# The two products of x with the first layer's weights: two groups of 256-column matmuls, or one group of 512 columns over two shared banks

## The reference, cut to what matters

```
deg = jnp.sum(adj, axis=-1, keepdims=True)
agg = jnp.einsum('bij,bjf->bif', adj, x) / jnp.maximum(deg, EPS)
cat = jnp.concatenate([x, agg], axis=2)
out = jnp.einsum('bnf,of->bno', cat, W)      # W is 256 x 512
return jax.nn.relu(out)
...
x = _layernorm(x + _L0_gnn_ref(x, adj, L0_gnn_W), axis=-1)
```

## Time and profile before

| | us |
|---|---|
| median of 3 runs | 1295.62 |
| lowest, highest | 1294.18, 1297.25 |
| span of the profiled execution | 1294.0 |
| PE busy | 1276.6 (99%) |
| PE weight loads busy | 1173.7 (91%) |
| DVE busy | 1194.4 (92%) |
| ACT busy | 909.7 (70%) |
| POOL busy | 140.6 (11%) |

### The profile page before, as it was taken

One profiled execution on the slowest core, in us unless ns is written; L12 is line 12 of the kernel. 1 busy time (PEld: TensorE's weight loads), 2 busy tenths in 40 slices (PEclk: granted clock), 3 DMA queues, 4 the chain that ended last, 5 costly groups with the idle time before them and its releaser, 6 DMA issues.

```text
span 1294.0 us, 30492 instructions
## 1 busy us (share of the span) xinstructions
PE 1276.6 (99%) x10976; PEld 1173.7 (91%) x10976; DVE 1194.4 (92%) x3789; ACT 909.7 (70%) x2445; POOL 140.6 (11%) x265
## 2 busy tenths in 40 slices
PE   7999999999999999999999999999999999999997
PEld 7899999999999999999999999999999999999986
DVE  6988999999999999999999999999999999999996
ACT  7677767677667677677677676776676776776773
POOL 0100111101111101111101111011111011110011
PEclk9999999999999999999999999999999999999999
DMA  6110111110111110111100111101111101110000
GB/s 227 34 35 1 35 43 44 43 43 2 43 43 43 43 40 4 44 43 43 43 24 21 43 43 44 43 3 43 43 43 43 36 8 43 43 43 9 10 9 25
DMA packets 34307, 49.01 MB, mean 38 GB/s; under 512 B 7920, under 2 KB 16880, under 8 KB 34160
## 3 DMA queue, kind: packets, MB, share of 16 engines
q1 hardware_dynamic: 34160, 47.08, 11.6%
HBM read 38.68 MB, written 8.39 MB: 36 GB/s over the span
## 4 chain that ended last, share of the span: by engine, by line
PE 96%; DVE 1%; DMA 1%; ACT 1%; POOL 0%; issue 0%; SPq 0%; POOLq 0%; DVEq 0%
PE psum L1487 63%; PE psum L1501 13%; PE psum L1742 9%; PE psum L1700 8%; PE psum L1793 1%; PE psum L1796 1%; PE psum L1805 1%; DMA adjT_sb<-in_adjT 1%; PE psum L1816 0%; DMA v_sb<-in_w 0%; DVE bn L869 0%; POOL rstd L347 0%; POOL mv L344 0%; DVE x L903 0%; DVE w_l L840 0%
## 5 line engine op out<-in xcount | busy, mean ns | idle before, releaser
L536 ACT ACTIVATE work<-work,shift 128x256 f32<-128x256 f32 x512 | 253.7, 498 | 37.6 <-DVE shift L1032 37.6
L1051 DVE SCALAR_TENSOR_TENSOR work<-work,rsum,extra 128x256 f32<-128x256 f32 x512 | 216.7, 475 | 0.1
L1032 DVE CUSTOM_DVE_ANT_0 work<-psum,minus_big 128x256 f32<-128x256 f32 x512 | 189.4, 416 | 1.8 <-PE psum L1700 1.8
L387 ACT ACTIVATE work<-psum 128x512 f32<-128x512 f32 x256 | 138.1, 596 | 73.9 <-PE psum L1501 70.0
L387 ACT ACTIVATE sup_h<-psum 128x512 fp32r<-128x512 f32 x124 | 73.5, 593 | 142.6 <-PE psum L1487 142.4
L344 POOL TENSOR_TENSOR mv<-mv,eps 128x2 f32<-128x2 f32 x128 | 33.1, 259 | 1139.3 <-DVE mv L890 1139.3
L1487 PE MATMUL psum<-x2T_h,wqkv_h 128*128 128x256 f32 x512 | 146.3, 286 | 0.0
L1487 PE MATMUL psum<-x2T_l,wqkv_h 128*128 128x256 f32 x512 | 142.8, 279 | 0.0
L1487 PE MATMUL psum<-x2T_h,wqkv_l 128*128 128x256 f32 x512 | 142.8, 279 | 0.0
L1501 PE MATMUL psum<-ident,work 128*128 128x128 f32 x1024 | 129.0, 274 | 0.0
L1742 PE MATMUL psum<-work,v_sb 128*64 128x256 f32 x1024 | 124.6, 385 | 0.0
(11 more groups left out here) (156 smaller groups left out, 3738.9 us busy)
## 6 DMA issues: line engine op xcount, KB each, us to landing
xT_sb<-in_xT SPq DMA_DIRECT2D x32, 256.0 KB, 2.6
adjT_sb<-in_adjT SPq DMA_DIRECT2D x32, 256.0 KB, 3.0
adj_sb<-in_adj SPq DMA_DIRECT2D x32, 256.0 KB, 4.5
x_sb<-in_x SPq DMA_DIRECT2D x32, 256.0 KB, 4.7
out<-y_sb SPq DMA_DIRECT2D x32, 256.0 KB, 4.5
work<-in_wqkv SPq DMA_DIRECT2D x1, 1536.0 KB, 10.8
mask_row<-in_nodemask SPq DMA_DIRECT2D x32, 32.0 KB, 4.5
w_raw<-in_w SPq DMA_DIRECT2D x3, 256.0 KB, 7.0
```

What stands on the lines that cost most here:

```text
L387: return nc.scalar.activation(dst, src, ACT.Copy, scale=scale)
L536: last = nc.scalar.activation(prob[:, p % 2, i, h], prob[:, p % 2, i, h], ACT.Exp, bias=shift[:, p % 2, h, i:i + 1], scale=-1.0, accum_out ...
L1032: last = V_.tensor_tensor_reduce(out=prob[:, p % 2, i, h], in0=bank(SCORES[p] + h)[:, i * N:(i + 1) * N], in1=minus_big[:, g % 2, i], scal ...
L1051: last = V_.scalar_tensor_tensor(out=prob[:, p % 2, i, h], in0=prob[:, p % 2, i, h], scalar=rsum[:, p % 2, h, i:i + 1], in1=extra[:, g % 2 ...
```

## The change

The two products are computed together. The weights of own part and support already lie side by side (`w0` has 512 columns), so one matmul now has 512 moving columns: the first node tile writes bank 0, the second bank 2, each with the own part in columns 0 to 255 and the support in 256 to 511. `support0` and `self_product` become `front_product`, with one semaphore `pe_front` at its end. ACT's `self_copy` moves to right behind `sup0_hi`, ahead of `values`. Both copies and DVE's `sup0_lo` now read a half of either bank, and `sup0_lo` waits for `self_copy` too.

```
-        SUP0 = 0
-        SELF = 2
+        FRONT = (0, 2)
+        OWN, SUPPORT = 0, 1
...
+        def front(part):
+            return psum[:, FRONT[0]:FRONT[1] + 1:FRONT[1] - FRONT[0], part * F:(part + 1) * F]
...
                 else:
                     reuse(act, pe_gcn, once(g - 1))
-                    act.wait_ge(pe_sup0, once(g))
-                copy(sup_of(g)[0][:, :, :], halves(bank(SUP0))).then_inc(act_sup0, 1)
+                    act.wait_ge(pe_front, once(g))
+                copy(sup_of(g)[0][:, :, :], front(SUPPORT)).then_inc(act_sup0, 1)
...
-                act.wait_ge(pe_self, once(g))
+                act.wait_ge(pe_front, once(g))
                 reuse(act, dve_agg, once(g - 1))
-                copy(self_part[:, :, :], halves(bank(SELF))).then_inc(act_self, 1)
+                copy(self_part[:, :, :], front(OWN)).then_inc(act_self, 1)
...
                 sup_hi(2, s - 1)
                 sup0_hi(s)
+                self_copy(s)
                 values(s - 2)
-                self_copy(s)
...
                 dve.wait_ge(act_sup0, once(g))
-                lo(sup_of(g)[1][:, :, :], halves(bank(SUP0)), sup_of(g)[0][:, :, :]).then_inc(dve_sup0, 1)
+                dve.wait_ge(act_self, once(g))
+                lo(sup_of(g)[1][:, :, :], front(SUPPORT), sup_of(g)[0][:, :, :]).then_inc(dve_sup0, 1)
...
-            def support0(g, part):
+            def front_product(g, part):
                 if not live(g):
                     return
                 if part == HI:
-                    weights(g, W0)
+                    weights(g, W0 + 1)
                     reuse(pe, act_oT, nth(g - 3, 3))
                     pe.wait_ge(act_xT, once(g))
                     reuse(pe, dve_oT, nth(g - 3, 3))
+                    reuse(pe, act_self, once(g - 1))
+                    if g == 2:
+                        reuse(pe, act_x1T, once(g - 1))
+                        reuse(pe, dve_x1T, once(g - 1))
+                    else:
+                        reuse(pe, dve_scores, nth2(g - 2, 0, 1))
                 else:
                     pe.wait_ge(dve_xT, once(g))
-                last = nodes_product(bank(SUP0), fT_of(g), [w[:, :, F:2 * F] for w in w0], part)
+                x = fT_of(g)
+                for t in range(NT):
+                    last = product(bank(FRONT[t]), [(cut(x, A, k, block_of(t)), cut(w0, A, k)) for k in range(FT)],
+                                   LEFT_LATE[part], opens=part == HI, closes=part == LO)
                 if part == LO:
-                    last.then_inc(pe_sup0, 1)
+                    last.then_inc(pe_front, 1)
...
+                    if p == 3:
+                        pe.wait_ge(act_self, once(g + 2))
...
                 qk(s - 3, 2)
-                support0(s - 1, HI)
+                front_product(s - 1, HI)
                 hidden(1, s - 2, HI)
                 hidden(1, s - 2, LO)
-                support0(s - 1, LO)
-                self_product(s - 1)
+                front_product(s - 1, LO)
                 project_out(s - 4, HI)
```

More of the change, by code:

```diff
@@ L191, in graph_blocks_kernel @@
         pool_var, pool_rstd = sems("pool_var", 4), sems("pool_rstd", 4)
-        (pe_mask, pe_w0, pe_w3, pe_xT, pe_adjT, pe_sup0, pe_self, pe_agg, pe_x1T, pe_gcn, pe_x2T, pe_v,
+        (pe_mask, pe_w0, pe_w3, pe_xT, pe_adjT, pe_front, pe_agg, pe_x1T, pe_gcn, pe_x2T, pe_v,
          pe_qk, pe_scores, pe_probT, pe_pv, pe_y, pe_x3T, pe_proj3, pe_adjk, pe_gate_row, pe_gate_col) = (
-            sem(n) for n in ("pe_mask", "pe_w0", "pe_w3", "pe_xT", "pe_adjT", "pe_sup0", "pe_self", "pe_agg",
+            sem(n) for n in ("pe_mask", "pe_w0", "pe_w3", "pe_xT", "pe_adjT", "pe_front", "pe_agg",
                              "pe_x1T", "pe_gcn", "pe_x2T", "pe_v", "pe_qk", "pe_scores", "pe_probT", "pe_pv",
@@ L630, in first_graphs @@
                 sup0_hi(0)
+                self_copy(0)
                 x_hi(1)
                 degrees(0)
-                self_copy(0)
                 mask_bias(0)
@@ L665, in first_graphs @@
                 sup0_hi(2)
+                self_copy(2)
                 adj_exp(2)
@@ L668, in first_graphs @@
                 qk_hi(0, 1)
-                self_copy(2)
                 sup_hi(1, 1)
@@ L717, in first_graphs @@
                 exps(1, 1, 1)
-                self_copy(3)
                 sup_hi(2, 2)
                 sup0_hi(3)
+                self_copy(3)
                 values(1)
@@ L758, in first_graphs @@
                 hidden_hi(1, 3)
-                self_copy(4)
                 adj_exp(4)
@@ L763, in first_graphs @@
                 sup0_hi(4)
+                self_copy(4)
                 values(2)
@@ L1870, in first_graphs @@
             def first_graphs():
-                support0(0, HI)
-                support0(0, LO)
-                self_product(0)
+                front_product(0, HI)
+                front_product(0, LO)
                 aggregate(0, HI)
                 aggregate(0, LO)
-                support0(1, HI)
-                support0(1, LO)
-                self_product(1)
+                front_product(1, HI)
+                front_product(1, LO)
                 keep_busy(7, 4)
@@ L1894, in first_graphs @@
                 x1_transpose(1)
-                support0(2, HI)
                 support(2, 0, HI)
@@ L1900, in first_graphs @@
                 gcn_out(0, LO)
-                support0(2, LO)
-                self_product(2)
+                front_product(2, HI)
+                front_product(2, LO)
                 support(0, 1, HI)
@@ L1955, in first_graphs @@
                 project_out(0, HI)
-                support0(3, HI)
                 project_out(0, LO)
-                self_product(3)
                 support(2, 2, HI)
@@ L1962, in first_graphs @@
                 gcn_out(2, HI)
-                support0(3, LO)
+                front_product(3, HI)
+                front_product(3, LO)
                 gcn_out(2, LO)
```

## The result

| | before | after |
|---|---|---|
| median of the runs, us | 1295.62 | 1311.62 (1310.74 to 1312.26) |
| span of the profiled execution, us | 1294.0 | 1309.0 |
| gcn_out to gcn_out in a slot, median | 39.27 | 39.71 |

The change makes the kernel slower: the ratio, against the runs of before on the same chip, is 1.0119, with a 95% interval of 1.0107 to 1.0131. The forecast was 1303.3 us with a range up to 1310.0. The direction was right; the loss is twice the forecast, 16.0 us for 7.7 (15.0 us by the spans; 15.7 by the medians if a fourth run of before, which the result lists, is counted in: 1295.9). The granted clock is again full (0.999).

The account below looks back on a forecast made before the run. The prediction took PE's instruction list and stalls as the bound, with DVE also on the path. Product -0.9, wait +8.1 and start +0.5 gave +7.7 us, 1303.3 us from 1295.6, range 1296.5 to 1310.

Parts of the forecast that it names:

- What bounds the kernel: Whole span: PE, busy 99%, sets the time by its instruction list plus whatever makes it stand; DVE is also on the path.
- The loop over DVE's `x2_lo`: PE releases `gcn_out`, DVE needs 10.4 us to `x2_lo`, PE takes over at `qk(·,0)`; closes once a slot, about no slack.
- Product, -0.03 us a graph: First-layer products on PE: 12 matmuls of 512 columns replace 24 of 256, 2.76 for 2.79 us; -0.9 us over 32 graphs.
- The wait, +0.29 us a slot, +8.1: DVE's `sup0_lo` waits for ACT's second copy, 0.51 us late; PE then 0.29 us late, 8.1 us over 28 slots.
- The restart of 0.11 us: PE at `aggregate LO`: restarting after standing 0.18 us costs 0.11 us more, making it 0.29 us late.
- `hidden(1)` and all other groups, 0: `hidden(1)` ends about 0.9 us later, covered by idle time on ACT and DVE; moved work costs nothing.
- The start, +0.5 (0 to 3): Graph 0: PE cannot begin with half the weights and support comes later, about 1.5 us hidden by a DMA wait; +0.5 us.
- The end, 0: Behind the last slots: the forecast's sum had no term for the end of the kernel.
- rival 3: DVE's whole delay is paid: 0.51 to 0.62 us a slot, +14 to +17, about 1310 us; chance 0.12.
- the gap: DVE's 0.23 us ahead of `aggregate`, waiting for `self_part`; the earlier copy removes it, leaving DVE 0.28 us late.
- Rival 1: The wait at `sup0_lo` is covered by DVE's gap and PE's slack: no change, 1295.2 us; chance 0.12.
- Rival 2: Fewer, longer matmuls on PE are really cheaper, 20 ns on each of 384 pairs, -7.7 us; about 1290 us; chance 0.08.

Follow-up runs that it names:

- e4: Before, with ACT copying the own part ahead of the support in the slots; 1294.78 us, ratio 1.0000.
- e3: Before with PE's new order in 256-column matmuls, a bank per product; PE's new wait ahead of `qk(·,3)` left in; 1313.37 us, ratio 1.0144.
- e5: After, with ACT copying the own part ahead of the support in the slots, in two one-bank pieces; single run, 1302.71 us.
- e2: Before, with the own part copied right behind the support and DVE's `sup_l` waiting for that copy, PE's list unchanged; 1307.16 us, ratio 1.0097.
- e6: After, with the low part of the front product as eight matmuls of 256 columns, high part still 512; 1311.64 us, ratio 1.0130.
- e9: After, with only the start reordered: `front_product(3)` high part ahead of `support(2, 2)`, low part behind `gcn_out(2, LO)`; 1311.33 us, ratio 1.0115.
- e7: e3 without PE's wait for the own part's copy ahead of `qk(·,3)`; 1300.66 us, ratio 1.0043.
- e8: After, with the early own-part copy of e5 and the 256-column low part of e6 together; 1302.82 us, ratio 1.0059.
- e10: After, with the early own-part copy of e5 and the reordered start of e9 together; 1301.86 us, ratio 1.0040.

## Why the prediction was wrong, step by step

- **What bounds the kernel.** PE, right. The loop over DVE's `x2_lo` was read too strictly. DVE arrives there with PE, but e4 shows that an earlier DVE shortens nothing. The 0.23 us to the second matmul of `qk(·,0)`, read in the earlier trace rows as the mark of a wait for DVE, is hardly one: it is still 0.21 us in e4, where `x2_lo` is done 0.20 us ahead. The loss of the wait goes through PE itself, late from `aggregate LO` on, as the bare stall of e3 shows.
- **Product, -0.03 us a graph.** The number came true in part by luck: 4.15 for 4.18 us with `hidden(1)`, 0.231 us for a matmul of 512 columns. But the products alone took 2.78 us for 2.77, and the gain is the shorter distance within `hidden(1)`, which the forecast held fixed.
- **The wait, +0.29 us a slot, +8.1.** Right in mechanism and nearly in size. `sup_l` was to be 0.51 us late and was 0.55: from the end of ACT's copy to the start of `sup_l` it took 0.10 us, not 0.05. The restart of 0.11 us was there (226 ns to the second matmul behind the stall, instead of 117), though it was taken from the earlier trace rows, where most of it is no restart. PE is 0.33 us late behind it, and e5 puts the wait at 0.34 us a slot, 9.1 us over 26 slots. That only +0.29 stand at the first product is no recovery: e5, which has no stall, is ahead of before there by the same 0.04 us. The last distance adds 0.6 us to the 9.1.
- **`hidden(1)` and all other groups, 0.** This step failed. I varied the distance of the new matmuls alone ("were the new pace 10 ns off") and took all others as fixed. They were not: 36 unchanged matmuls at 117.8 instead of 113.3 ns are +0.16 us a slot, 4.2 us over 26 slots, and they keep that distance when the wait is gone (e5). The earlier trace rows held the sign: 36 matmuls at 116 ns, beside the 113.3 of the 36 that follow them. Why the distance changes stays open.
- **The start, +0.5 (0 to 3).** The term for graph 0 was right at its low end, since the first `gcn_out` is not late. The loss is in the four distances that follow, +2.6 us, which I had not worked out graph by graph, so this term was too small by 2 us, though inside its bounds. 1.15 of it is `front_product(3)` standing whole between the two parts of `gcn_out(2)`, which I had in the diff. The wait by itself makes 0.7 of the 2.6 (e2).
- **The end, 0.** +0.8 us. From the 31st `gcn_out` to the end it is 101.89 us before and 102.66 after. The other traces tell where it comes from: 102.5 to 102.6 in the kernels that keep DVE's wait (e2, e6, e9), 102.45 with PE's stall (e3), and 101.9 to 102.1 without either (e4, e5, e7, e8, e10). So nearly all of it goes with the wait.

Sum in the slots: 9.1 (wait) + 4.2 (distance) - 0.8 (product, 26 x 0.03) - 1.0 (0.04 us a slot by which e5 is ahead of before at the first product) = 11.5, against 11.7 measured. Of the 7.3 us by which the span grew more than forecast (15.0 for 7.7), 4.2 are the distance, 2.0 the start and 1.6 the wait (9.7 for 8.1), less the 1.0.

The time fell where rival 3 was put, but not by its mechanism: `aggregate` on DVE was 0.33 us late, not 0.51 to 0.62, so the gap took its part (it was 0.16 us in e4, not 0.23). Rival 1 falls with the waits after. Rival 2 falls with the 0.231 us.

## What to carry to other kernels

A copy pair whose first half releases a reader should not get a second release for the sake of a shared bank, unless the second copy can be made ahead of the first. The new wait cost 9 to 10 us and the merged matmuls brought next to nothing (2.78 us for 2.77). If the busiest engine is full, ask of a new wait first whether that engine's next instruction comes late. And allow for unchanged work in the range: here 4.5 ns on each of 36 matmuls a slot made 4 us, half of the forecast's price for the wait.

## What the hardware showed that was not expected

In the stretches read here, PE's matmuls of 256 columns at a full clock mostly stand at one of two distances, 113.3 or 117.8 ns, and keep it for many matmuls in a row (36 and more). The same group with the same operands has one distance in one kernel and the other in the next (`project_out` and `support(2)`: 113.3 in before, e2, e3, e4 and e7; 117.8 in after, e5, e6, e8, e9 and e10). It repeats from slot to slot: these 36 take 4.08 us in each of the 25 slots of before from the sixth `gcn_out` on, and 4.24 in each of after. That speaks for what ran ahead as the cause, but it is argued, not shown. The change from slow to fast often comes with a step of 121 to 124 ns, but such a step also stands inside slow stretches, and one change in before goes 119, 116, 114 without it. Steps of 512 columns are 225 to 236 ns.

The Trainium skill (TensorE: Matmul & The Clock Gate, section "Wait — 56ns, not 53.3ns?") gives one distance for back-to-back matmuls on a warm array, N columns at 2.4 GHz plus about 2.5 ns. By it 256 columns would be an estimated 109.2 ns and 512 columns 215.8. The traces don't agree: 113.3 or 117.8, and 225 to 236, with a weight load for every matmul (10592 of each). What sets the distance was not found. e7 against e8 shows only that it can hang on how eight matmuls are formed, in width or in banks, 20 matmuls earlier.
